# One layer of a selective scan on eight cores: sixteen weight casts from GpSimd to VectorE, and four scans issued before the last items of an output stage

## The reference

```python
delta = softplus(xn @ Wd.T + bd)
a_pos = softplus(a_log) + 1e-4                      # [1024, 16]
# over time t, for each channel and each of 16 states:
state = exp(-delta_t * a_pos) * state + delta_t * b_param * xn_t
y_t   = state.sum(-1)
attn  = y @ Wo.T + bo
real  = xn @ cos(theta + theta_noise)
imag  = xn @ sin(phi + phi_noise)
out   = x + attn + sqrt(real**2 + imag**2)
```

## Time and profile before

| | us |
|---|---|
| median of 2 runs (1103.77 to 1104.43) | 1104.1 |
| the profiled execution | 1103.56 |
| span of its slowest core, core 1 | 1101.8 |
| spans of the eight cores | 1093.3 to 1101.8 |
| DVE busy | 816.5 (74%) |
| ACT busy | 582.3 (53%) |
| PE busy | 576.9 (52%) |
| POOL busy | 173.5 (16%) |

### The profile page before, as it was taken

One profiled execution on the slowest core, in us unless ns is written; L12 is line 12 of the kernel. 1 busy time (PEld: TensorE's weight loads), 2 busy tenths in 40 slices (PEclk: granted clock), 3 DMA queues, 4 the chain that ended last, 5 costly groups with the idle time before them and its releaser, 6 DMA issues.

```text
span 1101.8 us, 9309 instructions; the slowest of 8 cores (1093.3 to 1101.8 us)
## 1 busy us (share of the span) xinstructions
PE 576.9 (52%) x2248; PEld 240.5 (22%) x2248; DVE 816.5 (74%) x705; ACT 582.3 (53%) x924; POOL 173.5 (16%) x143
## 2 busy tenths in 40 slices
PE   1333244445467563555545447656556554465785
PEld 1211011112123230222211114433222211121343
DVE  4279988888843449999999992434899999999423
ACT  5784767766733235656665553332466655565330
POOL 2467800000012100000000001120000000000232
PEclk9855555566679765666665668897766666566799
DMA  8878500000013300000000001241100000000023
GB/s 237 225 205 221 139 0 1 0 0 1 0 48 95 91 33 0 1 1 0 1 0 1 0 0 54 84 128 45 43 1 1 0 1 1 0 0 1 29 73 114
DMA packets 36324, 51.65 MB, mean 47 GB/s; under 512 B 3120, under 2 KB 19760, under 8 KB 36272
## 3 DMA queue, kind: packets, MB, share of 16 engines
q1 hardware_dynamic: 33584, 42.68, 13.9%
q0 software_dynamic: 2688, 8.39, 2.3%
HBM read 42.67 MB, written 8.39 MB: 46 GB/s over the span
## 4 chain that ended last, share of the span: by engine, by line
DVE 41%; PE 21%; issue 17%; ACT 16%; DMA 3%; DVEq 1%; SPq 0%; ACTq 0%; POOL 0%; POOLq 0%
DVE grot L761 35%; ACT abar L715 9%; PE pd L884 6%; PE pt L607 3%; PE pd L296 3%; PE pt L617 3%; DVE sfm L898 2%; ACT bdg_bf L177 2%; DMA xsub<-xin 1%; PE pe L377 1%; PE py L912 1%; DMA sfm<-xin 1%; ACT L750 1%; DVE xsub L439 1%; PE pt L377 1%
## 5 line engine op out<-in xcount | busy, mean ns | idle before, releaser
L761 DVE TENSOR_TENSOR_SCAN grot<-abar,gcar,vbuf 128x768 bf16<-128x768 f32 (+1 forms) x384 | 662.4, 1786 | 42.3 <-ACT abar L715 33.5
L715 ACT ACTIVATE abar<-delta,nega 128x768 f32<-128x768 f32 (+1 forms) x384 | 340.4, 896 | 247.5 <-DVE grot L761 245.3
L799 PE MATMUL py<-grot,bdg_bf 128*128 128x384 bf16 x256 | 86.6, 445 | 119.6 <-DVE grot L761 119.5
L799 PE MATMUL pe<-grot,bdg_bf 128*128 128x384 bf16 x256 | 86.1, 441 | 119.6 <-DVE grot L761 119.5
L296 PE MATMUL pd<-xnbf,wd_bf 128*128 128x384 bf16 (+1 forms) x368 | 98.7, 449 | 20.6 <-ACT xsub L315 14.7
L658 POOL TENSOR_TENSOR xsub<-r,i 128x384 f32<-128x384 f32 (+1 forms) x9 | 18.1, 2008 | 364.8 <-ACT i L650 364.8
L786 PE MATMUL py<-grot,bdg_bf 128*128 128x512 bf16 x64 | 34.1, 546 | 76.4 <-DVE grot L761 76.4
L884 PE MATMUL pd<-ybf,wo_bf 128*128 128x384 bf16 (+1 forms) x320 | 72.3, 376 | 0.0
L607 PE MATMUL pt<-xnbf,cos_bf 128*128 128x384 bf16 (+1 forms) x320 | 72.3, 375 | 0.0
L786 PE MATMUL pe<-grot,bdg_bf 128*128 128x512 bf16 x64 | 34.4, 547 | 71.2 <-DVE grot L761 71.2
L617 PE MATMUL pt<-xnbf,sin_bf 128*128 128x384 bf16 (+1 forms) x320 | 65.3, 350 | 0.0
(11 more groups left out here) (107 smaller groups left out, 567.5 us busy)
## 6 DMA issues: line engine op xcount, KB each, us to landing
xsub<-xin SPq DMA_DIRECT2D x14, 512.0 KB, 4.4
xres<-xin SPq DMA_DIRECT2D x32, 192.0 KB, 2.4
out<-osub POOLq DMA_DIRECT2D x32, 192.0 KB, 2.6
xres<-xin SPq DMA_DIRECT2D x8, 256.0 KB, 3.9
out<-osub POOLq DMA_DIRECT2D x8, 256.0 KB, 3.3
etmp<-tht SPq DMA_DIRECT2D x6, 256.0 KB, 5.4
r<-thn SPq DMA_DIRECT2D x6, 256.0 KB, 5.4
r<-pht SPq DMA_DIRECT2D x6, 256.0 KB, 4.0
```

The costliest lines, as they stand in the source:

```text
L715: sx = run("scalar", lambda e, sl=sl_ab, par=par, dt=dt, n=n, tp=tp: e.activation(out=abar[:, sl * TP:sl * TP + tp], in_=delta[:, par * TP ...
L761: vs = run("vector", lambda e, g=gsl, sl=sl_ab, par=par, dt=dt, n=n, tp=tp: e.tensor_tensor_scan(out=grot[:, g * TP:g * TP + tp], data0=ab ...
L799: td = run("tensor", lambda e, c=c, g=gsl, dt=dt, n=n, bb=ypair[c]: e.matmul(bb[:, 0:384], bdg_bf[:, (dt * NST + n) * P:(dt * NST + n + 1) ...
```

## The change

1. The 16 casts of wo pieces to bf16 are issued on DVE in place of POOL, at the same places of the program: three each behind groups 1 to 4 of phase 0, four behind group 5. Each waits on DVE for its load. The next load into the slot waits for DVE, and so does the first FFN magnitude. ACT's wait for POOL's last cast in the FFN chain is left out.
2. In the output stage of phase 1, exponentials and scans 0 to 3 of group 0 of phase 2 are issued among the last items: exponential 0 behind item 12; scan 0, exponentials 1 and 2 and scan 1 behind item 13; exponential 3 and scan 2 behind item 14; scan 3 and the carry copy behind item 15. In phase 2's own loop they are skipped. The other work of that loop keeps its order, so the pieces that ACT does behind exponentials 1 to 3 come with no exponential between them.

The diff, cut (the skipped parts of the loop are the old code, indented under `if not hoisted`):

```diff
--- before.py
+++ after.py
         presp = [False] * (NPH + 1)
+        presc = [False] * (NPH + 1)
+        hoist_sx = {}
+        hoist_vs = {}
+
+        def emit_h_exp(pn, n):
+            tpn = TPL[pn]
+            sl = n % 3
+            for rj in {0: (11, 12), 1: (12, 13), 2: ()}[sl]:
+                wait("scalar", "V", ring_stt[rj])
+            wait("scalar", "V", ev_abar_free[sl])
+            wait("scalar", "S", sp_done[0])
+            sx = run("scalar", lambda e, sl=sl, n=n, tp=tpn: e.activation(
+                out=abar[:, sl * TP:sl * TP + tp],
+                in_=delta[:, 0:tp], func=AF.Exp,
+                scale=nega[:, n:n + 1]), "S")
+            hoist_sx[n] = sx
+            ev_delta_rd_s[0] = sx
+
+        def emit_h_scan(pn, n):
+            tpn = TPL[pn]
+            sl = n % 3
+            gsl = n % 4
+            wait("vector", "S", hoist_sx[n])
+            wait("vector", vv_done[0][0], vv_done[0][1])
+            wait("vector", "T", ev_g_free_t[gsl])
+            wait("vector", ev_g_free_v[gsl][0], ev_g_free_v[gsl][1])
+            vs = run("vector", lambda e, g=gsl, sl=sl, n=n, tp=tpn: e.tensor_tensor_scan(
+                out=grot[:, g * TP:g * TP + tp],
+                data0=abar[:, sl * TP:sl * TP + tp],
+                data1=vbuf[:, 0:tp],
+                initial=gcar[:, n:n + 1],
+                op0=ALU.mult, op1=ALU.add), "V")
+            hoist_vs[n] = vs
+            ev_abar_free[sl] = vs
+            ev_v_free[0] = vs
+            if n == 3:
+                wait("vector", "V", vs)
+                vc = run("vector", lambda e, tp=tpn: e.tensor_copy(
+                    out=gcar[:, 0:4],
+                    in_=grot[:].rearrange("q (s t) -> q s t", s=4)[:, :, tp - 1:tp]), "V")
+                for s4 in range(4):
+                    ev_g_free_v[s4] = ("V", vc)
 
         for p in range(NPH):
             tp = TPL[p]
...
                 wait("scalar", "V", winit_vec[0])
-                wait("scalar", "G", winit_last_g)
...
+                    hoisted = presc[p] and dt == 0 and n < 4
+                    if not hoisted:
...
+                    if hoisted:
+                        vs = hoist_vs[n]
...
                         sl, la, dst_, off_ = wo_pend.pop(0)
-                        wait("gpsimd", wsem[sl], la)
-                        g_ev = run("gpsimd", lambda e, d=dst_, o=off_, sl=sl: e.tensor_copy(
-                            out=d[:, o:o + 512], in_=wslot[sl]), "G")
-                        wfree[sl] = ("G", g_ev)
-                        winit_last_g = max(winit_last_g, g_ev)
-                        grp_done[id(dst_)] = ("G", g_ev)
+                        wait("vector", wsem[sl], la)
+                        v_ev = run("vector", lambda e, d=dst_, o=off_, sl=sl: e.tensor_copy(
+                            out=d[:, o:o + 512], in_=wslot[sl]), "V")
+                        wfree[sl] = ("V", v_ev)
+                        winit_vec[0] = v_ev
+                        grp_done[id(dst_)] = ("V", v_ev)
...
+                if p == 1:
+                    if it == 12:
+                        emit_h_exp(2, 0)
+                    elif it == 13:
+                        emit_h_scan(2, 0)
+                        emit_h_exp(2, 1)
+                        emit_h_exp(2, 2)
+                        emit_h_scan(2, 1)
+                    elif it == 14:
+                        emit_h_exp(2, 3)
+                        emit_h_scan(2, 2)
+                    elif it == 15:
+                        emit_h_scan(2, 3)
+                        presc[p + 1] = True
```

More of the change, by code:

```diff
@@ L706, in _build @@
                     gsl = n % 4
[L707 to L718, removed]
+                    hoisted = presc[p] and dt == 0 and n < 4
+                    if not hoisted:
+                        wait("scalar", "V", ev_abar_free[sl_ab])
+                        wait("scalar", "V", ev_init_v)
+                        wait("scalar", "S", sp_done[dt])
+                        if p == 0 and dt == 0 and n <= 1:
+                            wait("scalar", "T", ev_p0_slots.get(3, 0))
+                        if n <= 1:
+                            for rj in (11, 12, 13):
+                                wait("scalar", "V", ring_stt[rj])
+                        sx = run("scalar", lambda e, sl=sl_ab, par=par, dt=dt, n=n, tp=tp: e.activation(
+                            out=abar[:, sl * TP:sl * TP + tp],
+                            in_=delta[:, par * TP:par * TP + tp], func=AF.Exp,
+                            scale=nega[:, dt * NST + n:dt * NST + n + 1]), "S")
                     if n >= 1 and aux_i < len(aux):
@@ L756, in _build @@
                                 bdg_ev[adt] = ("S", ev_d)
[L757 to L775, removed]
+                    if hoisted:
+                        vs = hoist_vs[n]
+                    else:
+                        wait("vector", "S", sx)
+                        wait("vector", vv_done[dt][0], vv_done[dt][1])
+                        wait("vector", "T", ev_g_free_t[gsl])
+                        wait("vector", ev_g_free_v[gsl][0], ev_g_free_v[gsl][1])
+                        vs = run("vector", lambda e, g=gsl, sl=sl_ab, par=par, dt=dt, n=n, tp=tp: e.tensor_tensor_scan(
+                            out=grot[:, g * TP:g * TP + tp],
+                            data0=abar[:, sl * TP:sl * TP + tp],
+                            data1=vbuf[:, par * TP:par * TP + tp],
+                            initial=gcar[:, dt * NST + n:dt * NST + n + 1],
+                            op0=ALU.mult, op1=ALU.add), "V")
+                        ev_abar_free[sl_ab] = vs
+                        if n % 4 == 3:
+                            g0 = n - 3
+                            wait("vector", "V", vs)
+                            gs = grot[:].rearrange("q (s t) -> q s t", s=4)[:, :, tp - 1:tp]
+                            vc = run("vector", lambda e, a=gs, dt=dt, g0=g0: e.tensor_copy(
+                                out=gcar[:, dt * NST + g0:dt * NST + g0 + 4], in_=a), "V")
+                            for s4 in range(4):
+                                ev_g_free_v[s4] = ("V", vc)
```

## The result

| | us |
|---|---|
| before, median of 22 runs beside the changed kernel | 1104.3 |
| changed, median of 23 runs | 1109.3 |
| ratio changed / before | 1.0044, 95% interval 1.0031 to 1.0057 |
| span of the profiled execution, slowest core (core 0) | 1107.9 |
| the same kernel once more, in a later set, 12 runs beside 35 | 1.0019 (0.9995 to 1.0044) |

The changed kernel is slower by 0.4%, 4.9 us (3.4 to 6.3). The forecast was 1104.6 against 1104.1, so 0.5 us slower, in a range of 1100 to 1110.

What follows compares the result with a forecast made beforehand. VectorE was taken to bound the scan plateaus, with waits in the valleys between. From 1103.6 us, minus 2.3 relief, plus 1.4 casts and 1.4 hoist gave 1104.1, plus 0.5 for the median 1104.6 us; range 1100 to 1110.

Steps and rivals of the forecast that it cites:

- Relief from GpSimd: Phase 0 group 1: without GpSimd's casts, VectorE's scans and carry copies run shorter; gain 2.3 us, bounds 1.0 and 4.3.
- Price of the casts: Phase 0 group borders: casts at 0.49 us fill holes before scan 0; cost 1.4 us (0.8 plus 0.6 after group 5).
- Rival 2: Phase 0 group borders: each cast takes 0.69 us, casts cost 4.6 us, total 1107.8 us; chance 0.10.
- rival 4: Phase 0: VectorE's casts, and all scans behind them, wait for loads; then about 1127 us; chance 0.02.
- The hoist: Phase 1 to 2: item 15's sum and PE's queue run late, scan 4 waits for y matmuls; cost 1.4 us.
- some 14 us after scan 0: Head of phase 2: scan 4 waits for PE's py and starts at 784.7 against scan 0 at 770.6.
- the sentence on the clock: PE after 4 us idle before item 14: lower level for a while makes item 15's sum perhaps 0.2 us later.
- rival 3: Item 14 to y matmuls: PE stays at half rate behind the hoist, 5.2 us more, 1109.8 us; chance 0.10.
- the recovery after 735.33: PE woke after 4.38 us idle; its eight matmuls from 737.06 took 2.09 us, already a mix of both levels.
- The sum: Whole kernel: 1103.6 - 2.3 + 1.4 + 1.4 = 1104.1 us; median 0.5 above, so 1104.6 us.

Runs made afterwards that it cites:

- the run with throwaway matmuls: Changed kernel plus 20 unread matmuls keeping PE busy ahead of item 14's transposes in phase 1: 1104.5 us beside 1106.2, ratio 0.9991.
- y first: Changed kernel with the hoisted scans' eight y matmuls issued on PE ahead of phase 2's delta and FFN matmuls: 1109.5 us beside 1106.2, ratio 1.0039.
- y first with softplus late: Changed kernel, y matmuls ahead of delta, softplus pieces behind exponentials 6 to 9: 1103.0 us, ratio 0.9977; with 20 unread matmuls 1103.3 us, 0.9965.

## Why the forecast was right, and where it was off

**Relief from GpSimd: right, at the upper end.** Forecast 1.3 us up to scan 11 of group 1 and 1.0 behind it. From product 1 to product 2 the changed kernel is 2.1 us shorter on the mean core (37.7 to 35.6), but then scan 11 waits 3.09 us for ScalarE, where it waited 1.05. Product 2 is the first of these lines before and the second in the changed kernel, each from VectorE's timeline:

```profile
121.17 0.81 DVE L353 TENSOR_TENSOR vbuf<-delta,xn 128x640 f32<-128x640 f32 x1
```

```profile
119.01 0.82 DVE L353 TENSOR_TENSOR vbuf<-delta,xn 128x640 f32<-128x640 f32 x1
```

So scan 11 starts 127.27 - 119.01 = 8.26 us behind product 2, before 128.34 - 121.17 = 7.17. That leaves 1.0. From scan 11 to scan 0 of group 2 it is 136.29 - 127.27 = 9.02 us against 138.32 - 128.34 = 9.98: 1.0. Together 2.0 for a forecast 2.3, with ScalarE as the limit that was named. The other profiles with the casts on VectorE give from 1.1 to 2.5, and the eight together 1.6, because the time up to product 2 differs between cores. With the hoist alone, where GpSimd still casts, group 1 isn't shorter (37.8).

**Price of the casts: too high, and something else came in.** Forecast 0.49 us each, measured 0.42. The estimate from the Trainium skill's two elements a cycle (VectorE: DVE Perf Modes, The perf-mode tier table) gave 0.42, and the trace agrees. So three casts fit the hole of 0.94, and borders 1 to 4 cost nothing, where I had 0.8. The four casts behind group 5 make its border to group 6 0.34 us longer, where I had 0.6. Yet from product 6 to the last scan phase 0 takes 73.15 us on the mean core, before 72.18, so 0.97 more. The other 0.64 is two gaps of VectorE, ahead of scan 12 in groups 5 and 7, where no cast stands. This is the one in group 5, first before, then changed:

```profile
245.67 5.88 DVE L761 TENSOR_TENSOR_SCAN grot<-abar,gcar,vbuf 128x640 bf16<-128x640 f32 x4
```

```profile
243.96 5.88 DVE L807 TENSOR_TENSOR_SCAN grot<-abar,gcar,vbuf 128x640 bf16<-128x640 f32 x4 [0.42 <-DVE gcar L818]
```

The idle time ahead of the scan is 0.42 us (up to 0.44) in place of 0.10. It is so in both places on all eight cores of all eight profiles with the casts on VectorE, and on no core of the two profiles without. Each time a packet of 8192 bytes on a queue that the profile calls "instruction" comes 0.4 to 0.8 us behind that scan's start. Other gaps went away with the casts: scan 4 of group 0 of phase 1 idled 0.42 to 0.44 us with such a packet near it on all cores without them, and 0.10 with them. So the instructions added to VectorE's list seem to move such gaps, but no run here tests it. Sum 1.0 for a forecast 1.4, and net -1.0 for a forecast -0.9 (-0.1 to -1.5 in the eight profiles, -0.7 together): that they lie so close is in part luck, as 0.64 of the 1.0 is a term that the forecast didn't have. Rival 2 (0.69 us each) fell; so did rival 4: loads on SP's queue wait for VectorE, but no cast waits for a load.

**The hoist: the mechanism right, the term too small.** All steps show: item 15's sum is late, the delta matmuls and the FFN behind it too, scan 4 waits for PE's py. On cores that keep the full level, sum to scan 4 is 16.09 us (the run with throwaway matmuls, and core 4 of the changed kernel: 780.60 - 764.51 = 16.09), 0.85 later than before (1.1 than on its mean core), where I had 1.25. The sign "some 14 us after scan 0" holds there (14.1), and on core 0 it is 17.0. The step that failed is the sentence on the clock: I let PE be back at the full level by the delta matmuls and put 0.2 us for it. On five of eight cores these ran low for most of their length, 4.75 us instead of 2.76, and transposes and wo matmuls before them too: scan 4 came 3.74 us later, not 1.4. This is rival 3 at about half of its size, to which I gave 0.10. The measured 1109.3 lies within 1100 to 1110 only because the range took this rival in; the sum itself, +0.5, came out too low. My argument against it, the recovery after 735.33, was one core in one execution; the table shows that it goes either way, and the time is that of the slowest core, so one slow kind is enough.

**The sum.** By the stages of the mean core the first profile gives -1.0 us in phase 0 from product 1 on and +2.6 in the hoist stretch, so +1.6. The second gives -0.1 and +3.0, so +2.9, with the two cores of lower clock in it. The forecast had +0.5. The two comparisons measured +4.9 (3.4 to 6.3) and +2.1 (-0.6 to 4.9); they differ by 2.8 us, about as much as their intervals allow.

Every execution gives the spans of all eight cores, and their mean scatters less than the slowest of them. Over the executions behind the ratios of the two sets it moves by +2.4 us for the changed kernel, +3.6 for the hoist alone, -2.7 and -1.9 for the casts alone, -0.8 for the changed kernel with PE kept busy, +3.4 for y first, and -2.0 and -3.2 for y first with softplus late, without and with PE kept busy (each to about 1 us). That agrees with the stages for the hoist. For the casts the stages of their own two profiles give -1.5 and -0.8 from product 1 on, -0.35 in the scans of phase 1 (251.1 to 250.7) and -0.5 in the hoist stretch, so -2.3 and -1.8: the -1.0 above is not all of what the casts do. The moved gaps of VectorE lie in these two stretches too.

Why the first comparison reads +4.9 stays open. A part of it may be that the slowest core picks the slow kind: on its five cores the hoist stretch is 3.5 us longer. Another is seen but not explained: in each of the changed kernel's two profiles two cores spent 253.0 to 253.1 us in the scans of phase 1, where every other core of every kernel spent 250.5 to 251.2. Their granted clock from 420 to 660 us was 0.60, that of the other cores 0.62 or 0.63, and the hoist comes only later. Cores with a mean granted clock under 0.685 (a line drawn after the fact) stand in 17 of the 31 executions behind the ratios of the changed kernel, in 7 of 66 of the kernel before in the two sets and in 6 of 79 of the other seven runs. No run says why. And the stretch from phase 1's last scan to item 13's sum is 105.3 to 107.5 us on most cores and 108.7 to 112.3 on some. The latter is no work of the hoist: it shows on six of eight cores in the second run of the casts alone, and on none in the second profile of the changed kernel.

## What to carry to other kernels

To move work ahead into a valley, follow not the engine that gets it but what the work that it delays was releasing: here the four scans were done 1.0 us earlier, counted from item 13's sum, on core 0 and 2.0 on core 4, while item 15's sum, and PE's in-order queue behind it, came 4 us later. The hoist paid only with the queues behind it reordered too, PE's (y first) and ScalarE's (softplus later), and then by 0.7 to 1.2 us of the stage, which the time doesn't resolve. PE's alone was worth nothing; ScalarE's alone was not run. Taking work off GpSimd can be worth more in what it no longer disturbs on VectorE than the work costs there, if a hole of known cause is there to hold it.

## What the hardware showed beyond the expected

- The same idle time of PE, 3.59 us to the hundredth, in one execution of one program, left one core at the lower level and another at the full one. Over the four profiles that have this gap the transposes behind it ran low on 19 of 32 cores (5, 4, 6 and 4 of eight). A forecast of a stretch behind such a gap needs both values.
- At fixed places of the program VectorE idles 0.42 us ahead of a scan where it idles 0.10 otherwise, and an 8192-byte packet of an "instruction" queue follows the scan's start by 0.4 to 0.8 us. With sixteen more instructions in VectorE's list the places were others, the same on all eight cores.
- 20 matmuls that nobody reads, 3.41 us of them, made the stage faster by 1.6 us on the mean core. The ratio is 0.9991 (0.9970 to 1.0012), beside 1.0044 (1.0031 to 1.0057) and 1.0019 (0.9995 to 1.0044) for the same kernel without, each from another comparison; it is clear of the first and not of the second.
